# A two-layer model kernel on one core: its routed last pass on paired tiles with five groups added by rows, and its state-space stage written out

## The chip, the cores and the metric

One Trainium2 chip, one of its cores. The metric is the device time of one execution in microseconds (us). TensorE is PE in the profile, VectorE is DVE, ScalarE is ACT, GpSimd is POOL and SyncE is SP. SP and ACT also issue plain DMAs; POOL issues the indirect ones.

## The reference, cut to what matters

The input is x, f32 of shape (2, 4096, 512): 8192 tokens. Four blocks follow each other: a state-space block (projection, causal convolution, selective scan with 16 states per channel, gate, output projection, residual), a sum of eight orthogonal factors with a residual, a decayed linear attention with 16 heads, and a routed spline block. The change rewrites the end of the last one; of the state-space block it changes only how the code is written out:

```python
tile_idx = jnp.argmax(jnp.where(in_cluster, tile_scores, -jnp.inf), axis=-1)   # one of 64 tiles per token
tok_dims = DIMS[tile_idx]                                                      # the 8 features of that tile
x_slice = jnp.take_along_axis(xf, tok_dims, axis=1)
...
mn = tile_min[tile_idx][:, None]; mx = tile_max[tile_idx][:, None]             # over all tokens of the tile
u = jnp.clip((x_slice - mn) / (mx - mn + 1e-08), 0.0, 1.0 - 1e-06)
gi = jnp.clip((u * GRID).astype(jnp.int32), 0, GRID - 1)
b = spline_bases[tile_idx[:, None], j, gi]; s = spline_slopes[tile_idx[:, None], j, gi]
delta = (b + s * (u - gi / GRID) * GRID) * output_scale[tile_idx][:, None]
out = jnp.zeros_like(xf).at[jnp.arange(N)[:, None], tok_dims].set(delta)
return x + out.reshape(B, S, D)
```

The extremes of a tile need every token, so this end can only start when all tokens have been routed.

## The kernel before, in words

The program has three stages, one after the other, each in a block of its own with a barrier of all engines at its end. In all of them every engine's instructions are written out by hand in program order; engines meet by semaphores.

**State-space stage** (`mamba_block`). The sequence is cut in 16 chunks of 512 tokens (8 positions times batch 2). A chunk has 32 steps k; in each, PE builds the input term with `b_product` (L738: 16 matmuls of 32 x 128 weights, four row groups of the array at `tile_position=(32*i, 0)`), ACT the decays (L502), DVE four scans (L652), POOL the product with C (L336), and PE sums over states (L755). Projections, convolution and output projection of the neighbouring chunks lie between the steps by tables of step numbers. `y_out` (L601) of the last pair stands at step 1 of the following chunk. `periods` writes chunks 0, 1, 14 and 15 out and runs chunks 2 to 13 as a hardware loop of six turns with two chunks each, in which every semaphore wait compares with a value computed in registers:

```python
for b in range(BATCH):
    body(0, b, b, b == 0, False)
with eng.Fori(1, NI - 1) as i:
    for b in range(BATCH):
        body(i, b, i * BATCH + b, False, False)
```

**Second stage** (`blocks_after`): 64 tiles of 128 tokens in a software pipeline over the other blocks up to the routing. ACT issues the loads of the constants (18 DMAs, L1141 to L1145), DVE waits for all of them (L1234) and then sums and splits the weights, whose loads SP issues as buffers come free (L1059). It leaves in SBUF the one-hot of each token's tile (`oh_all`, bf16), the 8 picked features (`xs_all`) and the running extremes (`acc`), and stores `out` without the spline's delta (`r_t`, L1080).

**Last pass** (`finish`), L1663 and after, in 16 groups of four tiles:
- PE turns each tile's one-hot (L1803, 64 x 128 out of the 64-column weights), ACT evicts four at a time to `ohT` (L1693, 16 copies), in two alternating banks.
- DVE finds each token's tile number by multiplying the one-hot with 0..63 and reducing (L1701, L1708), so `rows` is known (L1712).
- PE looks up the two extremes of each token's tile (L1815, one matmul with 64-row weights per tile, two columns); DVE turns them into u, the cell and the remainder (L1725 to L1739).
- Per group: PE looks up 128 bases and 128 slopes per token (L1822, 8 matmuls), DVE marks the cells (`mark`, L1750), multiplies with the looked-up rows (`weigh`, L1760), reduces (`pick`, L1767), and forms delta (`slope` L1771, `offset` L1776).
- POOL issues one indirect DMA per tile (L1683), 64 in all, which adds 8 values per token into `out`; each group's four wait for that group's delta.

## Time and profile before

| | us |
|---|---|
| median of 3 executions | 5462.37 (5462.31 to 5465.17) |
| the profiled execution | 5468.6 |
| its span, first to last instruction | 5466.8 |
| state-space stage (0 to the barrier) | 3833 |
| second stage | 3833 to 5288 |
| last pass | 5288 to 5466.8 |

The busy shares over the span are PE 91%, DVE 82%, POOL 58%, ACT 48%. They are averages over three stages that differ, so each part is read in its own stretch. The granted TensorE clock is 1.0 (2.4 GHz) nearly everywhere in the first two stages and 0.5 (1.2 GHz) in the whole last pass. A matmul on f32 has two records in the trace.

### The profile page before, as it was taken

Reading aid. Unit: us, or ns where it says so; the run is one execution under the profiler, and the core shown is the slowest. Engines: PE = TensorE matmul, PEld = TensorE weight load, DVE = VectorE, ACT = ScalarE, POOL = GpSimd, SP = SyncE. Lnnn points to the kernel's source line nnn. Section 1 sums busy time; section 2 is a strip of 40 time slices with the busy share of each in tenths; the row PEclk is TensorE's granted clock in tenths of the full one; section 3 lists DMA queues with packets and bytes.
Section 4 is the critical chain, followed back from the end, with each engine's and each line's share of the span. In section 5 each row is a group of like instructions: output and inputs, shape, how many; then the busy total and the mean of one; then the engine's idle time right before and its main releaser. Section 6 shows DMA issues by size and latency. Waiting matters only on the chain. (4 is left out here: it accounts for less than half of the span.)

```text
span 5466.8 us, 107541 instructions
## 1 busy us (share of the span) xinstructions
PE 4975.0 (91%) x41287; PEld 2967.0 (54%) x41287; DVE 4462.5 (82%) x7277; ACT 2636.9 (48%) x4245; POOL 3175.6 (58%) x1659
## 2 busy tenths in 40 slices
PE   6899999999999999999999999987499999999983
PEld 3345444444444444444444445443388888888863
DVE  3988889888898888889888898886578888888864
ACT  3555556555565655556555565552133333333320
POOL 1676766767667676666766667675144444444427
PEclk9999999999999999999999999998799999999975
DMA  2222212222122222222222222221300000000001
GB/s 83 82 88 81 102 65 101 92 80 101 71 101 80 91 92 75 99 79 93 99 73 100 80 86 97 74 94 68 127 25 27 27 27 27 27 27 27 27 13 2
DMA packets 114433, 384.29 MB, mean 70 GB/s; under 512 B 29184, under 2 KB 30720, under 8 KB 81024
## 3 DMA queue, kind: packets, MB, share of 16 engines
q1 hardware_dynamic: 101600, 373.47, 19.3%
q0 software_dynamic: 9216, 0.27, 0.5%
q8 instruction: 340, 5.57, 0.4%
q10 hardware_dynamic: 3104, 3.58, 0.2%
q14 instruction: 173, 1.42, 0.1%
HBM read 342.92 MB, written 34.34 MB: 69 GB/s over the span
## 5 line engine op out<-in xcount | busy, mean ns | idle before, releaser
L336 POOL TENSOR_TENSOR s<-s,Cb 128x1024 f32<-128x1024 f32 x1024 | 2394.9, 2361 | 1084.2 <-DVE state L657 1073.8
L652 DVE TENSOR_TENSOR_SCAN s<-s,state,BU 128x512 f32<-128x512 f32 x2048 | 2452.8, 1260 | 426.5 <-PE BU L738 393.4
L502 ACT ACTIVATE s<-dt,ch 128x512 f32<-128x512 f32 x2048 | 1305.5, 712 | 780.4 <-PE Y L755 779.0
L755 PE MATMUL Y<-s,ident 64*64 64x512 f32 x8192 | 1014.9, 611 | 76.2 <-POOL s L336 75.2
L684 PE MATMUL PJ<-xnT,w_in 128*128 128x512 f32 x2048 | 946.1, 606 | 9.3 <-ACT dtuT L368 5.7
L738 PEld LDWEIGHTS BU<-spread,dtuT 32*128 32x128 f32 x16384 | 513.3, 189 | 527.7 <-DVE s L652 399.3
L738 PE MATMUL BU<-spread,dtuT 32*128 32x128 f32 x16384 | 611.9, 286 | 144.0 <-DVE s L652 139.6
L684 PEld LDWEIGHTS PJ<-xnT,w_in 128*128 128x128 f32 x2048 | 369.7, 190 | 478.5 <-issue 423.4
L755 PEld LDWEIGHTS Y<-s,ident 64*64 64x64 f32 x8192 | 279.7, 134 | 573.6 <-issue 535.7
L729 PE MATMUL PJ<-w_out,u 128*128 128x512 f32 x1024 | 472.3, 605 | 8.2 <-ACT xnT L372 6.7
L729 PEld LDWEIGHTS PJ<-w_out,u 128*128 128x128 f32 x1024 | 184.9, 190 | 243.3 <-issue 225.5
L1101 POOL TENSOR_TENSOR x1t<-x1t,bias_b 128x512 f32<-128x512 f32 x64 | 83.0, 1297 | 397.6 <-DVE xa L1285 397.6
L545 DVE SCALAR_TENSOR_TENSOR u<-hid,ch,u 128x512 f32<-128x512 f32 x384 | 287.5, 749 | 19.1
L695 PE MATMUL PJ<-w_xp,u 128*128 128x160 f32 x1024 | 252.9, 404 | 9.6 <-issue 6.5
L1106 POOL TENSOR_TENSOR xf<-xf,gamma_b 128x512 f32<-128x512 f32 x64 | 81.7, 1276 | 305.6 <-DVE xf L1472 305.6
L695 PEld LDWEIGHTS PJ<-w_xp,u 128*128 128x128 f32 x1024 | 243.0, 329 | 27.2 <-issue 20.8
L1481 DVE TENSOR_TENSOR scm<-bank,decay 128x512 f32<-128x512 f32 x256 | 159.0, 683 | 70.1 <-PE bank L1590 70.1
L1114 POOL TENSOR_TENSOR qk_all<-rc,rs 128x512 f32<-128x512 f32 x64 | 82.1, 1283 | 170.8 <-DVE rs L1499 170.8
L368 ACT COPY dtuT<-PJ 128x512 f32<-128x512 f32 x128 | 68.8, 588 | 230.6 <-PE PJ L724 230.6
L1551 PE MATMUL bank<-w_high_o,aTs 128*128 128x512 f32 x512 | 179.9, 412 | 0.0
L1551 PE MATMUL bank<-w_high_f,xaT 128*128 128x512 f32 x512 | 177.0, 407 | 1.6 <-DVE xaT L1290 1.4
L1290 DVE TENSOR_TENSOR xaT<-bank,xaT 128x512 fp32r<-128x512 f32 x64 | 44.3, 691 | 161.3 <-ACT xaT L1157 161.3
(238 smaller groups left out, 7095.1 us busy)
## 6 DMA issues: line engine op xcount, KB each, us to landing
Cb<-bc SPq DMA_DIRECT2D x256, 1024.0 KB, 4.8
res<-in_x SPq DMA_DIRECT2D x64, 256.0 KB, 4.8
x<-res SPq DMA_DIRECT2D x64, 256.0 KB, 4.9
x1t<-x SPq DMA_DIRECT2D x64, 256.0 KB, 2.6
out<-r_t SPq DMA_DIRECT2D x64, 256.0 KB, 2.0
xt<-in_x SPq DMA_DIRECT2D x31, 512.0 KB, 5.7
w_in<-in_in_w SPq DMA_DIRECT2D x8, 512.0 KB, 9.6
x_all<-in_factors SPq DMA_DIRECT2D x4, 1024.0 KB, 5.1
```

The source lines that it names most:

```text
L336: nc.gpsimd.tensor_tensor(pair, pair, Cb[q % 2][:, 2 * part * T:2 * part * T + 2 * T], ALU.mult).then_inc(z_ready, 1)
L502: nc.scalar.activation(s[k % SLOTS][:, n, :], dt[p % 2][:, gi, :], ACT.Exp, scale=ch[:, 2 * p + gi, 7 + 4 * nq + n:8 + 4 * nq + n]).then_i ...
L545: last_ = nc.vector.scalar_tensor_tensor(out, h_[:, tap:tap + T], ch[:, m, tap:tap + 1], out, ALU.mult, ALU.add)
L652: nc.vector.tensor_tensor_scan(s[k % SLOTS][:, n, :], s[k % SLOTS][:, n, :], BU[:, n::4], state[:, b, k, n:n + 1], ALU.mult, ALU.add).then ...
L684: last_ = nc.tensor.matmul(bank[:], w_in[:, kb, lo:lo + P], xnT[:, kb, :], start=(kb == 0), stop=(kb == KB - 1))
L695: last_ = nc.tensor.matmul(bank[:, tb % 2 * SP_:(tb % 2 + 1) * SP_], by_block(u[slot][:, g, :])[:, tb], w_xp[:, g, :], start=(g == 0), sto ...
L729: last_ = nc.tensor.matmul(bank[:], u[slot][:, g, j * P:(j + 1) * P], w_out[:, g, :], start=(g == 0), stop=(g == G - 1))
L738: last_ = nc.tensor.matmul(BU[:, i * T:(i + 1) * T].rearrange("p (t b n) -> p b t n", b=TB, n=4)[:, tb], dtuT[rows, gi, tb, :], spread[row ...
L755: last_ = nc.tensor.matmul(Y[r][y_rows(r, gi), :], ident[rows, rows], s[(k_even + gi) % SLOTS][rows, n, :], start=False, stop=(n == 3 and ...
L1101: nc.gpsimd.tensor_tensor(x1t[s_][:], x1t[s_][:], bias_b[:], ALU.add).then_inc(S["x1b_ready"], 1)
L1481: nc.vector.tensor_tensor(scm[:, r, :, :].rearrange("p k n -> p (k n)"), bank(f"sc{r}")[:], decay[:, r, :, :].rearrange("p k n -> p (k n)" ...
L1551: last_ = nc.tensor.matmul(b_[:], src[part][:, k, :], wt, start=(k == 0 and i == 0), stop=(k == KB - 1 and i == 2))
```

## The change

Three edits.

1. `periods` writes all 16 chunks out; the loop is gone, and with it the register values in the waits.
2. The last pass works on pairs of tiles. One matmul turns the one-hots of two tiles, so a transposed block has 128 partitions, tile 2p in partitions 0 to 63 and tile 2p+1 in 64 to 127. The tables (`tab`, `oscale`, the extremes) stand in both halves, and the look-ups alternate between the two row halves of the array (`tile_position=(64*r, 0)`), each half with its own PSUM bank; bases and slopes come from one matmul of 256 columns. The tile number is a third column of the extremes' look-up, which replaces the multiply-and-reduce on DVE. The load of the tables needs two more DMAs on ACT's queue.
3. Groups 11 to 15 are no longer scattered. SP reads their rows of `out` (10 DMAs of 512 KB) at the start of the pass, DVE spreads delta over the 512 features by the one-hot (`to_rows`) and adds (`add_rows`), and SP stores the rows. POOL issues 44 indirect DMAs.

The buffers of the last pass are allocated anew after the second stage's are released.

```diff
         def periods(eng, body):
 
-            for b in range(BATCH):
-                body(0, b, b, b == 0, False)
-            with eng.Fori(1, NI - 1) as i:
-                for b in range(BATCH):
-                    body(i, b, i * BATCH + b, False, False)
-            for b in range(BATCH):
-                body(NI - 1, b, (NI - 1) * BATCH + b, False, b == BATCH - 1)
+            for c in range(NCH):
+                body(c // BATCH, c % BATCH, c, c == 0, c == NCH - 1)
...
-            act.dma_start(tab[:, 0, :], w["bases"].rearrange("a j g -> a (j g)")).then_inc(S["w_loaded2"], 16)
-            act.dma_start(tab[:, 1, :], w["slopes"].rearrange("a j g -> a (j g)")).then_inc(S["w_loaded2"], 16)
+            for h in range(2):
+                both = slice(NTILE * h, NTILE * h + NTILE)
+                for q, src in enumerate(("bases", "slopes")):
+                    act.dma_start(tab[both, q, :], w[src].rearrange("a j g -> a (j g)")).then_inc(S["w_loaded2"], 16)
...
-            dve.wait_ge(S["w_loaded2"], 16 * 18)
+            dve.wait_ge(S["w_loaded2"], 16 * 20)
...
+    BY_ROWS = 5
+    SCATTERED = GROUPS - BY_ROWS
...
+        @block.sync
+        def _(sp):
+            for i in range(BY_ROWS):
+                for b in range(2):
+                    sp.dma_start(rows_of[i][:, b::2, :],
+                                 out_v[b, of_group(SCATTERED + i)].rearrange("i p d -> p i d")).then_inc(rows_loaded, 16)
+            for i in range(BY_ROWS):
+                sp.wait_ge(rows_added, i + 1)
+                for b in range(2):
+                    sp.dma_start(out_v[b, of_group(SCATTERED + i)].rearrange("i p d -> p i d"),
+                                 rows_of[i][:, b::2, :]).then_inc(rows_stored, 16)
+            sp.wait_ge(rows_stored, 32 * BY_ROWS)
 
         @block.gpsimd
...
-            for t in range(TILES):
+            for t in range(SCATTERED * N):
-            pool.wait_ge(scattered, 16 * TILES)
+            pool.wait_ge(scattered, 16 * SCATTERED * N)
...
-            nc.scalar.copy(ident_b[:], ident[:]).then_inc(ident_ready, 1)
-            for g in range(GROUPS):
-                act.wait_ge(oh_turned, g + 1)
-                nc.scalar.copy(ohT(g * N, N), banks[g % 2][0:NTILE, :]).then_inc(ohT_ready, 1)
+            for h in range(GROUPS // 2):
+                act.wait_ge(oh_turned, h + 1)
+                nc.scalar.copy(ohT(h * N, N), banks[h % 2][:]).then_inc(ohT_ready, 1)
...
+            nc.vector.tensor_copy(ident_b[:], ident[:]).then_inc(ext_column, 1)
+            for q in range(2):
+                nc.vector.tensor_copy(twice[:, q, :].rearrange("p (h i) -> p h i", h=2),
+                                      ident[:, q * NTILE:(q + 1) * NTILE].unsqueeze(1).to_broadcast([P, 2, NTILE])
+                                      ).then_inc(ext_column, 1)
+            nc.vector.tensor_copy(ext[:, 2:3], tile_no[:]).then_inc(ext_column, 1)
...
-            half = TILES // 2
-            for h in range(2):
-                nc.vector.tensor_tensor(
-                    marked[h][:].rearrange("p k (t i) -> p (k t) i", i=NTILE), oh[:, h * half:(h + 1) * half, :],
-                    buf["tile_no"][:].unsqueeze(1).to_broadcast([P, half, NTILE]), ALU.mult).then_inc(marked_ready, 1)
             dve.wait_ge(ext_full, 1)
-            nc.vector.tensor_copy(ext[:], banks[6][0:NTILE, 0:2]).then_inc(ext_ready, 1)
-            for h in range(2):
-                dve.wait_ge(marked_ready, h + 1)
-                nc.vector.tensor_reduce(idx[:, h * half:(h + 1) * half],
-                                        marked[h][:].rearrange("p k (t i) -> p (k t) i", i=NTILE), AX.X, ALU.add
-                                        ).then_inc(idx_step, 1)
-            dve.wait_ge(idx_step, 2)
-            nc.vector.tensor_tensor(rows[:], idx, buf["row_base"][:], ALU.add).then_inc(rows_ready, 1)
+            nc.vector.tensor_copy(ext[:, 0:2], banks[7][:, P:P + 2]).then_inc(ext_ready, 1)
 
             steps = itertools.count(1)
...
+            for r in range(2):
+                nc.vector.tensor_copy(e[:, r, :], banks[6 + r][:, 0:3 * TILES // 2]).then_inc(chain, 1)
+                next(steps)
+            dve.wait_ge(chain, 2)
+            e_q = e[:].rearrange("p r (t q) -> p t r q", q=3)
+            by_pair = rdn[:].rearrange("p (t r) -> p t r", r=2)
+            nc.vector.tensor_tensor(rows[:].rearrange("p (t r) -> p t r", r=2), e_q[:, :, :, 2],
+                                    row_base[:].rearrange("p (t r) -> p t r", r=2), ALU.add).then_inc(rows_ready, 1)
+            then(nc.vector.tensor_tensor(by_pair, e_q[:, :, :, 0], e_q[:, :, :, 1], ALU.add))
+            then(nc.vector.tensor_scalar_add(rdn[:], rdn[:], 1e-8))
+            for r in range(2):
+                def half(ap):
+                    return per_dim(ap).rearrange("p (t r) j -> p t r j", r=2)[:, :, r, :]
+                nc.vector.tensor_tensor(half(v16[:]), xs[:].rearrange("p (t r) j -> p t r j", r=2)[:, :, r, :],
+                                        e_q[:, :, r, 1].unsqueeze(2).to_broadcast([P, TILES // 2, DS]), ALU.add)
+            then(nc.vector.reciprocal(rdn[:], rdn[:]))
+            then(nc.vector.tensor_tensor(per_dim(v16[:]), per_dim(v16[:]), spread(rdn[:]), ALU.mult))
...
-            def weigh(g, q):
-                if q == 0:
+            def weigh(g, r):
+                if r == 0:
                     dve.wait_ge(eq_ready, g + 1)
...
-                nc.vector.tensor_tensor(prod[q][:], eq[g % 2][:], banks[2 * (g % 2) + 2 + q][:], ALU.mult
-                                        ).then_inc(prod_ready, 1)
-
-            def pick(g, q):
-                dve.wait_ge(prod_ready, 2 * g + 1 + q)
+                    dve.wait_ge(picked, 2 * (g - 1) + 1 + r)
+                marks = eq[g % 2][:].rearrange("p (t r c) -> p t r c", r=2, c=P)[:, :, r, :]
+                nc.vector.tensor_tensor(prod[r][:].rearrange("p (t q c) -> p t q c", q=2, c=P),
+                                        marks.unsqueeze(2).to_broadcast([P, 2, 2, P]),
+                                        banks[2 * (g % 2) + 2 + r][:].rearrange("p (t q c) -> p t q c", q=2, c=P),
+                                        ALU.mult).then_inc(prod_ready, 1)
...
+            def to_rows(g):
+                i = g - SCATTERED
+                if i >= 2:
+                    dve.wait_ge(rows_added, i - 1)
+                dve.wait_ge(delta_ready, g + 1)
+                nc.vector.tensor_tensor(od[i % 2][:].rearrange("p t (i j) -> p t i j", j=DS),
+                                        oh[:, g * N:(g + 1) * N, :].unsqueeze(3).to_broadcast([P, N, NTILE, DS]),
+                                        per_dim(of(delta, g)).unsqueeze(2).to_broadcast([P, N, NTILE, DS]), ALU.mult
+                                        ).then_inc(od_ready, 1)
+
+            def add_rows(g):
+                i = g - SCATTERED
+                dve.wait_ge(rows_loaded, 32 * BY_ROWS)
+                dve.wait_ge(od_ready, i + 1)
+                nc.vector.tensor_tensor(rows_of[i][:], rows_of[i][:], od[i % 2][:], ALU.add).then_inc(rows_added, 1)
...
                     offset(g - 1)
                 pick(g, 1)
+                if g > SCATTERED:
+                    to_rows(g - 1)
+                if g > SCATTERED + 1:
+                    add_rows(g - 2)
             slope(GROUPS - 1)
+            add_rows(GROUPS - 2)
             offset(GROUPS - 1)
+            to_rows(GROUPS - 1)
+            add_rows(GROUPS - 1)
 
...
-            for g in range(GROUPS):
-                if g >= 2:
-                    pe.wait_ge(ohT_ready, g - 1)
-                for t in range(g * N, (g + 1) * N):
-                    last_ = nc.tensor.matmul(banks[g % 2][0:NTILE, t % N * P:(t % N + 1) * P], oh[:, t, :], ident_b[:],
+            pe.wait_ge(ext_column, 1)
+            for h in range(GROUPS // 2):
+                if h >= 2:
+                    pe.wait_ge(ohT_ready, h - 1)
+                for n in range(N):
+                    pair = h * N + n
+                    last_ = nc.tensor.matmul(banks[h % 2][:, n * P:(n + 1) * P],
+                                             oh[:, 2 * pair:2 * pair + 2, :].rearrange("p t i -> p (t i)"), ident_b[:],
                                              start=True, stop=True)
                 last_.then_inc(oh_turned, 1)
-                if g == 1:
-                    pe.wait_ge(ext_column, 1)
+                if h == 1:
+                    pe.wait_ge(ext_column, 5)
                     for q in range(2):
-                        last_ = nc.tensor.matmul(banks[6][0:NTILE, q:q + 1], ident[:, q * NTILE:(q + 1) * NTILE],
-                                                 ext_T[:], start=True, stop=True)
+                        last_ = nc.tensor.matmul(banks[7][:, P + q:P + q + 1], twice[:, q, :], ext_T[:],
+                                                 start=True, stop=True)
                     last_.then_inc(ext_full, 1)
             pe.wait_ge(ext_ready, 1)
-            pe.wait_ge(ohT_ready, GROUPS)
-            for t in range(TILES):
-                last_ = nc.tensor.matmul(banks[6][:, 2 * t:2 * t + 2], ohT(t), ext[:], start=True, stop=True)
+            pe.wait_ge(ohT_ready, GROUPS // 2)
+            pe.sem_inc(pe_steps3, 1)
+            for pair in range(TILES // 2):
+                for r in range(2):
+                    half = slice(NTILE * r, NTILE * r + NTILE)
+                    last_ = nc.tensor.matmul(banks[6 + r][:, 3 * pair:3 * pair + 3], ohT(pair)[half, :], ext[half, :],
+                                             start=True, stop=True, tile_position=(NTILE * r, 0))
             last_.then_inc(e_full, 1)
             for g in range(GROUPS):
                 if g >= 2:
                     pe.wait_ge(prod_ready, 2 * (g - 2) + 2)
-                for q in range(2):
-                    for t in range(N):
-                        last_ = nc.tensor.matmul(banks[2 * (g % 2) + 2 + q][:, t * P:(t + 1) * P], ohT(g * N + t),
-                                                 tab[:, q, :], start=True, stop=True)
+                    pe.sem_inc(pe_steps3, 1)
+                for n in range(2):
+                    for r in range(2):
+                        half = slice(NTILE * r, NTILE * r + NTILE)
+                        last_ = nc.tensor.matmul(banks[2 * (g % 2) + 2 + r][:, 2 * n * P:2 * n * P + 2 * P],
+                                                 ohT(2 * g + n)[half, :], tab[half].rearrange("a q c -> a (q c)"),
+                                                 start=True, stop=True, tile_position=(NTILE * r, 0))
                 last_.then_inc(looked_up, 1)
```

On PE, the last pass from the transpose of the extremes on; before:

```order
L1796 MATMUL bank<-ident,acc 128x128
L1803 MATMUL bank<-x1t,oh_all 64x128 x8
L1809 MATMUL bank<-x1t,ident 64x1 x2
L1803 MATMUL bank<-x1t,oh_all 64x128 x56
L1815 MATMUL bank<-x1t,x_all 128x2 x16
L1815 MATMUL bank<-x1t,qk_all 128x2 x16
L1815 MATMUL bank<-x1t,scm 128x2 x16
L1815 MATMUL bank<-x1t,decay 128x2 x16
L1822 MATMUL bank<-tab,x_all 128x128 x32
L1822 MATMUL bank<-tab,qk_all 128x128 x32
L1822 MATMUL bank<-tab,scm 128x128 x32
L1822 MATMUL bank<-tab,decay 128x128 x32
```

and now:

```order
L1854 MATMUL bank<-ident,acc 128x128
L1862 MATMUL bank<-ident_b,oh_all 128x128 x8
L1869 MATMUL bank<-ext_T,twice 128x1 x2
L1862 MATMUL bank<-ident_b,oh_all 128x128 x24
L1878 MATMUL bank<-ext,ohT 128x3 x64
L1888 MATMUL bank<-tab,ohT 128x256 x64
```

The 64 transposes are 32, the extremes' look-ups keep their number and read three columns, and the 128 look-ups of the tables are 64 of twice the columns.

On DVE, the end of the last pass, from the second `weigh` and the last reductions on; before:

```order
L1767 TENSOR_REDUCE kTs<-xb 128x32
L1760 TENSOR_TENSOR xb<-xa,bank 128x512
L1771 TENSOR_TENSOR kTs<-kTs,x_0 128x32
L1760 TENSOR_TENSOR xb<-xa,bank 128x512
L1767 TENSOR_REDUCE kTs<-xb 128x32
L1776 TENSOR_TENSOR rc<-kTs 128x32
L1767 TENSOR_REDUCE kTs<-xb 128x32
L1771 TENSOR_TENSOR kTs<-kTs,x_0 128x32
L1776 TENSOR_TENSOR rc<-kTs 128x32
```

and now (`od` is delta spread to rows, `rows_of` the rows of `out`):

```order
L1805 TENSOR_TENSOR sel<-sel,v 128x4x8
L1790 TENSOR_TENSOR prod<-eq,bank 128x512
L1799 TENSOR_REDUCE sel<-prod 128x32
L1810 TENSOR_TENSOR delta<-sel 128x2x2x8
L1799 TENSOR_REDUCE sel<-prod 128x32
L1819 TENSOR_TENSOR od<-oh_all,delta 128x2048
L1828 TENSOR_TENSOR rows_of<-rows_of,od 128x2048
L1805 TENSOR_TENSOR sel<-sel,v 128x4x8
L1828 TENSOR_TENSOR rows_of<-rows_of,od 128x2048
L1810 TENSOR_TENSOR delta<-sel 128x2x2x8
L1819 TENSOR_TENSOR od<-oh_all,delta 128x2048
L1828 TENSOR_TENSOR rows_of<-rows_of,od 128x2048
```

Behind the group's own instructions stand products and sums of 2048 elements a partition, five of each in all; they are behind `pick` of groups 12 to 15 and at the end.

## Rows read from the trace of the kernel before

**Rows 1.** the page, its first line

```profile
span 5466.8 us, 107541 instructions
```

**Rows 2.** busy time by window: chunks 2 to 13, second stage, last pass

```profile
core 0: us, PE busy (x) PEld busy (x) DVE busy (x) ACT busy (x) POOL busy (x), PEclk, DMA share, GB/s
581.00:3349.00 2768.00, 2625.57 (x22753) 1301.29 (x22752) 2417.15 (x2941) 1632.46 (x2388) 1887.64 (x853) 1.00 0.25 88
3833.00:5288.00 1455.00, 1342.31 (x10498) 1121.82 (x10498) 1169.10 (x3225) 446.60 (x1027) 558.26 (x452) 0.96 0.11 36
5288.00:5467.00 179.00, 92.12 (x453) 89.05 (x453) 67.84 (x132) 8.79 (x17) 100.30 (x64) 0.50 0.15 2
```

**Rows 3.** timeline, DVE: gate multiply of chunks 1, 2, 3, 14, 15

```profile
362.07 1.26 DVE L601 TENSOR_TENSOR u<-Y,gate 128x512 f32<-128x512 f32 x2
591.48 1.26 DVE L601 TENSOR_TENSOR u<-Y,gate 128x512 f32<-128x512 f32 x2
821.67 1.26 DVE L601 TENSOR_TENSOR u<-Y,gate 128x512 f32<-128x512 f32 x2
...
3359.56 1.26 DVE L601 TENSOR_TENSOR u<-Y,gate 128x512 f32<-128x512 f32 x2
3588.68 1.26 DVE L601 TENSOR_TENSOR u<-Y,gate 128x512 f32<-128x512 f32 x2
```

**Rows 4.** the page: a queue that fetches instructions (packets, MB, share)

```profile
q8 instruction: 340, 5.57, 0.4%
```

**Rows 5.** timeline, ACT in the last pass: first and last evictions of one-hots

```profile
5289.28 1.06 ACT L1693 COPY x_all<-bank 64x512 f32<-64x512 f32 x2 [0.78 <-PE bank L1803]
...
5298.40 1.06 ACT L1693 COPY decay<-bank 64x512 f32<-64x512 f32 x2 [0.24 <-PE bank L1803]
```

**Rows 6.** groups by form: a quarter of the look-ups of the extremes

```profile
L1815 PE MATMUL bank<-x1t,scm 64*128 64x2 f32 x32 | 7.0, 349 | 0.0
```

**Rows 7.** timeline, PE: one 32-row tiled product of 16 matmuls at half clock

```profile
133.57 2.09 PE L738 MATMUL BU<-spread,dtuT 32*128 32x128 f32 x32 [4.99 <-DVE s L652]
```

**Rows 8.** timeline, DVE: range extremes arriving, last step before marking, group pace

```profile
5327.07 0.29 DVE L1725 COPY kTs<-bank 128x128 f32<-128x128 f32 x1 [28.96 <-PE bank L1815]
5333.82 1.29 DVE L1750 TENSOR_TENSOR xa<-x,grid 128x512 f32<-128x512 f32 x2
5340.61 0.68 DVE L1750 TENSOR_TENSOR xa<-x,grid 128x512 f32<-128x512 f32 x1
5343.79 0.68 DVE L1750 TENSOR_TENSOR xa<-x,grid 128x512 f32<-128x512 f32 x1
```

**Rows 9.** timeline, scatters: first two, a slow one, its mark, the last

```profile
5341.04 1.85 POOL L1683 DMA_INDIRECT out<-rc,x1t  x1 [59.63 <-DVE rc L1776]
5343.19 1.55 POOL L1683 DMA_INDIRECT out<-rc,x1t  x1 [0.30 <-issue]
...
5359.90 0.68 DVE L1750 TENSOR_TENSOR xa<-x,grid 128x512 f32<-128x512 f32 x1
5359.98 2.02 POOL L1683 DMA_INDIRECT out<-rc,x1t  x1 [0.30 <-issue]
...
5455.10 1.56 POOL L1683 DMA_INDIRECT out<-rc,x1t  x1 [2.00 <-issue]
5460.68 1.55 POOL L1683 DMA_INDIRECT out<-rc,x1t  x1 [0.30 <-issue]
```

**Rows 10.** groups of instructions by line, DVE, weight set-up (busy us, mean ns)

```profile
L1258 DVE TENSOR_TENSOR qk_all<-qk_all,scm 128x2048 f32<-128x2048 f32 x4 | 9.2, 2292 | 2.9 <-DMA scm<-in_factors 2.8
```

**Rows 11.** timeline, second stage: last constant load, and DVE's wait for it

```profile
3843.72 0.61 ACTq L1145 DMA_DIRECT2D tab<-in_slopes  x1
3850.10 0.28 DVE L1235 TENSOR_REDUCE smean<-tab 64x8 f32<-64x128 f32 x1 [19.55 <-DMA tab<-in_slopes]
```

**Rows 12.** DMA issues by line (KB each, median us to landing)

```profile
out<-r_t SPq DMA_DIRECT2D x64, 256.0 KB, 2.0
x_all<-in_factors SPq DMA_DIRECT2D x4, 1024.0 KB, 5.1
```

More of the change, by code:

```diff
@@ L898, in blocks_after, with keep @@
     ctx = ExitStack()
+    stage = ExitStack()
     with ctx:
         def sb(name, shape, dt=F32):
+            return stage.enter_context(nc.sbuf_tensor(name, shape, dt))
+        def keep(name, shape, dt=F32):
             return ctx.enter_context(nc.sbuf_tensor(name, shape, dt))
@@ L1644, in finish @@
[L1644 removed]
+        stage.close()
+        finish(nc, out, out_v, banks, dict(ident=ident, tab=tab, grid16=grid16, acc=acc, oh=oh_all, xs=xs_all,
+                                           row_base=row_base, tile_no=tile_no), NTILE, DS, GRID, TILES)
+def finish(nc, out, out_v, banks, kept, NTILE, DS, GRID, TILES):
     N = 4
     GROUPS = TILES // N
[L1648 to L1651 removed]
+    BY_ROWS = 5
+    SCATTERED = GROUPS - BY_ROWS
+    ident, tab, grid16, acc, oh, xs, row_base, tile_no = (
+        kept[n] for n in ("ident", "tab", "grid16", "acc", "oh", "xs", "row_base", "tile_no"))
@@ L1664, in sem @@
         def sem(name):
             return ctx.enter_context(nc.semaphore(name))
[L1667 to L1671 removed]
+        CELLS = TILES * DS
@@ new lines, in finish @@
+        ohT_all = [sb(f"ohT{i}", [P, TILES // 4 * P]) for i in range(2)]
+        rows_of = [sb(f"rows_of{i}", [P, N, NTILE * DS]) for i in range(BY_ROWS)]
+        od = [sb(f"od{i}", [P, N, NTILE * DS]) for i in range(2)]
+        eq, prod = ([sb(f"{n}{i}", [P, N * P]) for i in range(2)] for n in ("eq", "prod"))
+        v16, gf, gt, delta = (sb(n, [P, CELLS]) for n in ("v16", "gf", "gt", "delta"))
+        gi, rows = sb("gi", [P, CELLS], I32), sb("rows", [P, TILES], I32)
+        ident_b = sb("ident_b", [P, P], BF16)
```

89 lines of the change are left out of this document (39 added, 50 removed).

## The prediction

> **What bounds the kernel now.** I read the page's first line, then busy time by window, then the timeline of each stretch that the change touches. The span is 5466.8 us [rows 1]. Three stages follow each other behind barriers [rows 2], so what is saved in one is saved at the end.
>
> *State-space stage.* In chunks 2 to 13 PE is busy 2625.6 of 2768 us and DVE 2417 [rows 2]. The engines take turns in each step, so I don't look for one bound but for a yardstick: the gate multiply in step 1 of each chunk, one period apart. Chunks 1 and 14 are written out already, chunks 2 to 13 run in the loop. From chunk 1's row to chunk 2's is 229.41 us, from 14's to 15's 229.12; in the loop the first period is 230.19, and the twelve take 3359.56 - 591.48 = 2768.08 us, 230.67 each [rows 3].
>
> *Last pass.* PE and DVE have done most of it by 5387 us; from the first scatter at 5341.04 to the last one's end (5460.68 + 1.55 = 5462.23) POOL issues its 64 indirect DMAs, 1.55 us each with 0.30 between them [rows 9]. So the pass is a prologue of 53 us up to the first delta (barrier at 5288), then POOL's queue for 121.2 us, then 4.6 us of landing and ending. TensorE has 1.2 GHz throughout it [rows 2].
>
> **The change, part by part.**
>
> *Loop written out.* Nothing is computed differently; register arithmetic before the waits and the branch go. The price is read off the same code without a loop: the mean of the two written-out periods is 229.27, the loop's 230.67, so 12 x 1.40 = **-17 us** (by chunk 1 alone -15, by chunk 14 alone -19).
>
> *Two more loads in the second stage.* DVE waits for the last constant, 19.55 us of idle time ended by that load, which ACT issued at 3843.72 after one every half microsecond [rows 11]. Two more issues of about 0.6 come ahead of it, and the weights' setup hangs on that wait: **+1.2 us** (0 if another load would be last).
>
> *Transposes of one-hots.* 16 evictions take 5289.28 to 5298.40 + 1.06 = 5299.46 [rows 5], 0.64 each; PE and ACT alternate on two banks. Now there are 8; 128 columns of weights instead of 64 hide beside the 128 columns that pass, and an eviction of 128 partitions costs what one of 64 does. 5.1 us, and 0.3 for the longer product of the extremes that stands between: **-4.8**. The multiply and reduction of tile numbers lay beside this; with them gone nothing is won.
>
> *Look-ups of the extremes.* A quarter, 16 matmuls in 32 records, takes 7.0 us [rows 6], all 64 take 27.4; nothing else runs on the path. There are still 64, now alternating between row halves. How two halves overlap no row of this shape shows. Bounds: no overlap, 0 gained, and full overlap, 13.7. The nearest row: 16 matmuls of 32-row weights in four row groups take 2.09 us at the same clock [rows 7], 0.13 each against 0.44, 3.3 times as fast with four groups, loading of weights included. I take the full factor two for two groups: **-13.6**.
>
> *DVE up to the first delta.* From the extremes' arrival (5327.07) to the first mark (5333.82) it is a chain of short dependent operations [rows 8]. One copy becomes two, an addition for the row numbers and a second half-sized addition come in: **+0.5**. First mark and first delta follow as before. The first scatter is thus due at 5341.04 - 4.8 - 13.6 + 0.5 = 5323.1 (in the old time scale).
>
> *POOL.* 44 scatters at 1.85 us are 81.4, less the last gap 81.1. To this comes what DVE costs POOL. Of the 24 scatters issued while DVE works, most take 1.55 us, but one that starts 0.08 after a mark began takes 2.02 [rows 9]: it ends late by about what the mark had left. A mark has both inputs in SBUF; multiplies that read PSUM and reductions delay nothing. The new `to_rows` and `add_rows` have both inputs in SBUF, and 2048 elements of f32 take 2.29 us [rows 10], longer than POOL's 1.85 rhythm, so no scatter can slip between. They come mostly in pairs: a scatter that starts inside the first waits about 1.1 on average, the next falls into the second one's end and waits about 0.4. Five pairs, 7.5 us, and 1.5 for the marks. 81.1 + 9 = 90.1 against 121.2: **-31.1**. The 2.00 us pause before the 61st scatter [rows 9] is in the 121.2 and is assumed not to come with 44.
>
> The Trainium skill (SBUF — State Buffer, Who interferes with whom) says that a DVE instruction with two SBUF inputs contends with a GpSimd instruction that reads SBUF, and that the second to issue fully blocks; by that rule the trace agrees (2.02 against 1.55). The same page's warning on software-generated DMAs names only the two-port copies of DVE; by that alone `to_rows` and `add_rows` would cost POOL nothing, and the sum would be 7.5 us lower.
>
> *DVE's own end.* A group costs it 3.18 us (5340.61 to 5343.79) [rows 8]. First mark at 5333.82 - 17.9 = 5315.9, 16 groups 50.9, ten long operations at 2.21 net 22.1: 5389. PE's look-ups, 4 matmuls of 256 columns a group, take 3.4 us if the halves don't overlap and 1.7 if they do, so they hold DVE up little or not at all. The store of the last group, two DMAs of 512 KB, lands within 5.1 us (1 MB took that) [rows 12]: 5395. The last scatter ends at 5323.1 + 90.1 = 5413.2. POOL stays the bound, with 18 us of slack for DVE and SP. The 5 MB of rows read at the start take 5 x 5.1 = 26 us [rows 12], done by 5315 and first wanted after 5360. If scatters were free of DVE, the slack would still be 9 us.
>
> *Sum.* -17 + 1.2 - 4.8 - 13.6 + 0.5 - 31.1 = -64.8 us. The profiled execution took 5468.6 us, 1.8 over its span and 6.2 above the median of 5462.4; it becomes 5403.8, the median **5398 us**.
>
> **The rivals.**
>
> A. *Row halves do not overlap.* For: each f32 matmul passes twice (two records) through its own half before the next half's is issued, and no row has two row groups of 128 columns. Against: the four-group product. +13.6 on the path: 5411.
>
> B. *The long DVE operations don't hold POOL.* For: the evidence is a few scatters on one kind of instruction. Against: the delay follows the mark's remaining time. -7.5: 5390.
>
> C. *POOL is shut out over a whole pair*, since DVE's next operation is queued when the first ends. Marks were followed by PSUM readers, so the trace can't say. Another 2.2 us per pair less what the second wait already costs, five times, about +9: 5407.
>
> D. *Chunks 2 to 13 are slow for another reason than the loop.* For: chunks 1 and 14 lie at the ends. Against: the same instructions with registers in every wait. +17: 5415.
>
> E. *Slower than before: written-out code starves for instructions.* The larger fetch queue moved 5.57 MB in 340 packets [rows 4]; written out, the stage brings the code of ten more chunks that no turn repeats. If fetches were exposed, each of the 12 chunks would lose time; the kernel becomes slower by over 0.2% once a chunk loses (64.8 + 11) / 12 = 6.3 us against the loop-free 229.3. With 8 us each it would be 5494. Against: chunks 1 and 14 are fetched fresh, with no such loss, and the whole second stage is written out.
>
> **How the numbers follow.** What I forecast has 0.56, A 0.10, B 0.12, C 0.12, D 0.05, E 0.03; 0.02 is left for something that undoes the pass's gain altogether. The predicted time is the likeliest case's, 5398. Its own uncertainties are 2 us on the loop, 3 on how the scatters fall against DVE's operations, 2 on the pause: about 6. The range takes in B below and A and C above: 5385 to 5412. A difference under 0.2%, 11 us, is about what a measurement of this kernel cannot tell from none. All cases but E, and part of the last, are faster by more: faster 0.96, same 0.01, slower 0.03.
>
> **What the profile of the changed kernel would show.** Gate multiplies 229.1 to 229.4 us apart in all chunks; if 230.7, the loop was not the cause. The second stage about 1 us longer. Eight evictions in some 5.5 us; 64 look-ups of three columns in 13.8 us (A: 27.4). First scatter some 35 us after the barrier, not 53. Scatters of 1.55 us, and in the last third of DVE's work five or more of 2 to 3.5 us that start inside `to_rows` or `add_rows` (B: none; C: up to 5). DVE done about 24 us ahead of the last scatter. If the last store lands after the last scatter, or POOL waits for a delta, my reading of the bound is wrong.

## The result and the profile after

The changed kernel takes 5411.12 us (median of 4 runs, 5409.99 to 5414.31), the kernel before, run beside it, 5463.69 (4 runs, 5462.31 to 5465.17). The ratio is 0.9901, 95% interval 0.9888 to 0.9913: 52.6 us are gained. The prediction was 5398 with a range of 5385 to 5412, a gain of 64.4. The profiled execution took 5414.31 us.

First the page of the changed kernel, its span and its instruction queue (packets, MB, share), to be held against [rows 1, 4]:

```profile
span 5412.4 us, 102320 instructions
...
q8 instruction: 328, 5.37, 0.4%
```

Busy time by window, the three stretches that answer to [rows 2], moved to where the stages now lie:

```profile
core 0: us, PE busy (x) PEld busy (x) DVE busy (x) ACT busy (x) POOL busy (x), PEclk, DMA share, GB/s
581.00:3349.00 2768.00, 2640.32 (x22924) 1309.88 (x22923) 2436.72 (x2963) 1643.85 (x2404) 1901.05 (x860) 1.00 0.25 89
3813.00:5275.00 1462.00, 1348.96 (x10498) 1121.98 (x10499) 1171.32 (x3225) 446.58 (x1027) 557.32 (x452) 0.96 0.11 36
5275.00:5413.00 138.00, 51.67 (x293) 38.16 (x293) 80.95 (x144) 4.29 (x8) 84.21 (x44) 0.51 0.34 78
```

The second window spoils the forecast. The same number of matmuls (10498) and of DVE instructions (3225) fills 1462 us, where it filled 1455. Beyond the two loads, priced at 1.2 us, nothing that the diff above shows explains it.

*State-space stage.* The timeline of DVE, gate multiplies of chunks 1, 2, 3, 14 and 15, against [rows 3]:

```profile
362.48 1.26 DVE L596 TENSOR_TENSOR u<-Y,gate 128x512 f32<-128x512 f32 x2
591.65 1.26 DVE L596 TENSOR_TENSOR u<-Y,gate 128x512 f32<-128x512 f32 x2
821.05 1.27 DVE L596 TENSOR_TENSOR u<-Y,gate 128x512 f32<-128x512 f32 x2
...
3339.87 1.26 DVE L596 TENSOR_TENSOR u<-Y,gate 128x512 f32<-128x512 f32 x2
3568.72 1.27 DVE L596 TENSOR_TENSOR u<-Y,gate 128x512 f32<-128x512 f32 x2
```

The twelve chunks that the loop ran take 3339.87 - 591.65 = 2748.22 us, 229.02 each, against 2768.08 and 230.67. Code loading did not grow: 5.37 MB in 328 packets over the whole execution, against 5.57 MB in 340.

*Last pass up to the first scatter.* ACT's evictions (timeline), the look-ups of the extremes (groups by form, from 5275 to 5303), and DVE's first copy and first mark (timeline), against [rows 5, 6, 8]:

```profile
5275.95 1.07 ACT L1720 COPY ohT<-bank 128x512 f32<-128x512 f32 x2 [7.09 <-PE bank L1862]
...
5280.15 1.07 ACT L1720 COPY ohT<-bank 128x512 f32<-128x512 f32 x2 [0.21 <-PE bank L1862]
```

```profile
L1878 PE MATMUL bank<-ext,ohT 64*128 64x3 f32 x128 | 13.8, 350 | 0.7 <-issue 0.7
```

```profile
5295.18 0.42 DVE L1747 COPY e<-bank 128x96 f32<-128x96 f32 x2 [17.89 <-PE bank L1878]
...
5302.32 1.29 DVE L1778 TENSOR_TENSOR eq<-gf,grid 128x512 f32<-128x512 f32 x2
```

Eight evictions end at 5281.2 and 64 look-ups take 13.8 us instead of 27.4, a full factor of two. The look-ups alternate between two row halves and, with them, between two PSUM banks, where all wrote one bank before; no run separates the two.

*Last pass, scatters.* The timeline of POOL, first two scatters and last, against [rows 9]:

```profile
5309.52 1.86 POOL L1711 DMA_INDIRECT out<-delta,rows  x1 [41.32 <-DVE delta L1810]
5311.69 1.54 POOL L1711 DMA_INDIRECT out<-delta,rows  x1 [0.30 <-issue]
...
5405.29 1.54 POOL L1711 DMA_INDIRECT out<-delta,rows  x1 [0.30 <-issue]
```

From the first to the end of the last it is 97.3 us; 44 scatters without any wait would be 81.1. The 16.2 us that are missing come from places such as this one, in the timeline around one group by rows:

```profile
5348.77 1.54 POOL L1711 DMA_INDIRECT out<-delta,rows  x1 [0.30 <-issue]
...
5349.53 2.30 DVE L1819 TENSOR_TENSOR od<-oh_all,delta 128x2048 f32<-128x2048 bf16 x1
5350.62 5.44 POOL L1711 DMA_INDIRECT out<-delta,rows  x1 [0.30 <-issue]
5351.73 2.31 DVE L1828 TENSOR_TENSOR rows_of<-rows_of,od 128x2048 f32<-128x2048 f32 x1
5353.93 0.71 DVE L1778 TENSOR_TENSOR eq<-gf,grid 128x512 f32<-128x512 f32 x1
...
5354.53 0.70 DVE L1790 TENSOR_TENSOR prod<-eq,bank 128x512 f32<-128x512 f32 x1
...
5356.36 1.54 POOL L1711 DMA_INDIRECT out<-delta,rows  x1 [0.30 <-issue]
```

One scatter takes 5.44 us. It starts within `to_rows`, sits through `add_rows` and the mark behind it, and ends 1.42 us after the mark has ended (5354.64, against 5356.06): nearly a whole scatter's time after the end of the run (a row of operations with both inputs in SBUF, each of which starts some 0.1 us before the one ahead has ended). The next operation, which reads PSUM, doesn't disturb it.

Where the span went, before to after:

| stretch | before | after | change | predicted |
|---|---|---|---|---|
| end of the last scan | 3791.3 | 3771.3 | -20.0 | -17 |
| from there to the last pass's first transpose | 1496.9 | 1503.7 | +6.8 | +1.2 |
| to the first scatter | 52.8 | 34.5 | -18.3 | -17.9 |
| first scatter to the last one's end | 121.2 | 97.3 | -23.9 | -31.1 |
| to the end | 4.6 | 5.6 | +1.0 | 0 |
| span | 5466.8 | 5412.4 | -54.4 | -64.8 |

### The profile page after: what moved, and what is told of

It reads as the page before. It is cut to its first block and busy times, and to the rows that moved or that the text cites. A ratio compares the mean times of both kernels' runs of the same rounds, so it can differ in the third digit from the quotient of the medians.

```text
span 5412.4 us, 102320 instructions
## 1 busy us (share of the span) xinstructions
PE 4936.5 (91%) x41127; PEld 2916.7 (54%) x41127; DVE 4479.3 (83%) x7289; ACT 2633.0 (49%) x4236; POOL 3157.2 (58%) x1639
## 3 DMA queue, kind: packets, MB, share of 16 engines
q8 instruction: 328, 5.37, 0.4%
```

## Finding the second stage's 6 us

The second stage ran as a pipeline over 64 tiles. The timeline of DVE gives a mark once a tile, the statistics of a new tile. Tiles 8 and 56 in the kernel before:

```profile
4033.52 0.68 DVE L1273 BATCH_NORM_STATS2 st_a<-x1t 128x6 f32<-128x512 f32 x1
...
5043.89 0.68 DVE L1273 BATCH_NORM_STATS2 st_a<-x1t 128x6 f32<-128x512 f32 x1
```

and in the changed kernel:

```profile
4014.22 0.68 DVE L1274 BATCH_NORM_STATS2 st_a<-x1t 128x6 f32<-128x512 f32 x1
...
5029.59 0.68 DVE L1274 BATCH_NORM_STATS2 st_a<-x1t 128x6 f32<-128x512 f32 x1
```

That is (5043.89 - 4033.52) / 48 = 21.05 us a tile before and 21.15 after, evenly in all tiles. The granted clock is the same (0.96 in the windows). The tenth of a microsecond is found on PE, whose queue is full here (busy for 1003 of the 1015 us between these two tiles). In the kernel before, the 12 matmuls of the product for k start at even steps (timeline of PE):

```profile
4521.64 0.39 PE L1551 MATMUL bank<-w_high_k,xbT 128*128 128x512 f32 x1
4521.86 0.39 PE L1551 MATMUL bank<-w_low_k,xbT 128*128 128x512 f32 x1
...
4524.35 0.39 PE L1551 MATMUL bank<-w_high_v,xbT 128*128 128x512 f32 x1
```

and in the changed kernel the same 12 take 2.75 us, not 2.71:

```profile
4504.78 0.39 PE L1552 MATMUL bank<-w_high_k,xbT 128*128 128x512 f32 x1
4505.01 0.39 PE L1552 MATMUL bank<-w_low_k,xbT 128*128 128x512 f32 x1
...
4507.53 0.39 PE L1552 MATMUL bank<-w_high_v,xbT 128*128 128x512 f32 x1
```

Averaged over 43 tiles, the steps of the q product were 226.7, 226.6 and 226.6 ns (high to low, low to high, high to high) and are 225.8, 229.2 and 231.7: 6.8 ns for each three matmuls, some 0.08 us over the 36 of q, k and v in a tile. The instructions are the same. What the change did touch, in lines that the diff above leaves out, is where the tensors lie: the eight that outlive the stage are now allocated ahead of the weights, which moves the weights up by 12640 bytes, but `ones` and what follows it, the transposed blocks among them, by less, since ident, tab and grid16 no longer lie between. The blocks moved by 11040. Four of the experiments below are on this.

## The experiments

All are timed in five rounds beside the kernel before, whose median was 5464.9 us beside `pad_new`, `pad_old`, `unroll_only` and `no_rows`, 5465.9 beside `addr_old`, `dist_new`, `spread_rows` and `psum_od`, and 5466.7 beside `pieces` and the last two. Since the first stage alone ends up to 5 us apart from run to run of the same code, I read each cause from its own stretch of the trace and use the whole time only as a second witness.

**pad_new: everything 32 bytes higher.** Before the change the weights began at a multiple of 64 bytes, after it 32 bytes beside one.

```diff
         tile_no = keep("tile_no", [P, 1])
+        keep("pad", [P, 8])
```

> The changed kernel with 32 unused bytes allocated behind tile_no, so that every tensor of the second stage starts 32 bytes higher, at a multiple of 64 bytes as before the change (w_high_f at 29184 instead of 29152). Alignment theory: the q, k and v products start every 226.6 ns again instead of 225.8, 229.2 and 231.7 ns, each of the 64 pipeline tiles takes 21.05 us instead of 21.15, and the program gets 6 to 6.5 us faster, 5405 us. Rival, the cost lies in which tensors lie beside each other or in the instructions' own order: the tiles keep 21.15 us and the time stays at 5411.

5411.09 us, ratio 0.9899 (0.9884 to 0.9915): nothing gained. A tile takes 21.17 us, as long as in the changed kernel. The three steps of the q product became 231.5, 225.9 and 229.2 ns: the same three values with their places exchanged, the same sum. Addresses do something here, but alignment to 64 bytes is not it.

**pad_old: the kernel before, 32 bytes higher.**

```diff
+        sb("pad", [P, 8])
         w_high, w_low = ({n: sb(f"w_{part}_{n}", [P, KB, HID], F32R) ...
```

> The kernel before with 32 unused bytes allocated ahead of w_high_f, everything else as it was. Alignment theory: each of the 64 tiles takes 21.15 us instead of 21.05 and the program is 6 to 6.5 us slower, 5470 us. Rival as for the other padding: nothing changes, 5463.7 us.

5466.08 us, ratio 1.0002 (0.9993 to 1.0011), 21.05 us a tile, 226.7 ns a step. The theory of alignment fell in this direction too.

**unroll_only: the kernel before with `periods` written out.**

```diff
-            for b in range(BATCH):
-                body(0, b, b, b == 0, False)
-            with eng.Fori(1, NI - 1) as i:
...
+            for c in range(NCH):
+                body(c // BATCH, c % BATCH, c, c == 0, c == NCH - 1)
```

> The kernel before with only the state-space stage unrolled. Theory: the last scan ends 20 us earlier, as in the changed kernel, the second stage keeps its 21.05 us a tile and the last pass its length, so the program is 20 us faster, 5443.5 us. Rival, the unrolled instructions cost the second stage its 6 us (instruction supply): the gain is 14 us, 5450 us.

5444.96 us, ratio 0.9962 (0.9949 to 0.9976), 19.9 us less than before. The twelve chunks take 2747.4 us (2748.2 in the changed kernel), and the second stage keeps 21.05 us a tile and its steps of 226.6 ns. So neither a longer code nor where PE's instructions lie costs the 6 us.

**addr_old: the kernel before with the second stage's tensors where the changed kernel has them,** all up to the late ones behind `ts`. Instructions change in nothing but their addresses.

```diff
+        ident = sb("ident2", [P, P])
+        tab = sb("tab", [NTILE, 2, DS * GRID])
+        grid16 = sb("grid16", [P, GRID])
...
+        row_base = sb("row_base", [P, TILES])
+        sb("pad", [P, 1])
         w_high, w_low = ({n: sb(f"w_{part}_{n}", [P, KB, HID], F32R) ...
...
```

> The kernel before with its tensors allocated in the changed kernel's order, so that w_high_f starts at 29152, xbT0 at 158368 and all others of the second stage up to ts where they do in the changed kernel; no instruction changes but its addresses. Placement theory (which survives the failed padding: it is the distance between tensors that counts, not a multiple of 64 bytes): the tiles take 21.15 us instead of 21.05, 5471 us. Rival, the cost lies in the instruction streams of the changed kernel's second stage: the tiles keep 21.05 us, 5464.5 us.

5472.15 us, 6.3 more than before, ratio 1.0011 (1.0002 to 1.0020). The timeline of DVE, tiles 8 and 56:

```profile
4030.16 0.68 DVE L1274 BATCH_NORM_STATS2 st_a<-x1t 128x6 f32<-128x512 f32 x1
...
5045.52 0.68 DVE L1274 BATCH_NORM_STATS2 st_a<-x1t 128x6 f32<-128x512 f32 x1
```

21.15 us a tile, and steps of 226.0, 229.1 and 231.6 ns: the changed kernel's rate without any other part of the change. From the first tile's statistics to the last one's the profiled execution took 4.4 us more than the kernel before, the changed kernel 6.1; stretches of the same placement differ by up to 2 us from run to run, and the steady rate between tiles 8 and 56 is the firmer witness.

**dist_new: the changed kernel with the old distance from the weights to the transposed blocks.** Everything from rms_w on moves 1600 bytes up, away from the weights.

```diff
+        pr = sb("pr", [P, HID], BF16)
+        cs = sb("cs", [P, 8])
+        cm = sb("cm", [P, 8])
+        cand = sb("cand", [P, 2, NTILE])
         rms_w = sb("rms_w", [P, KB])
...
```

> The changed kernel with 1600 bytes of tensors that were allocated late (pr, cs, cm, cand) allocated between w_low_o and rms_w, so that the distance from each weight to x1t, xaT, xbT, aTs and everything between them is what it was before the change, all of them 12640 bytes higher. If the distance from the weights to the transposed blocks decides: 21.05 us a tile, 5405 us. If the addresses themselves decide, or the order of instructions: 21.15 us, 5411 us.

5404.53 us, 61.4 below the kernel before, ratio 0.9889 (0.9874 to 0.9905). Tiles 8 and 56:

```profile
4010.46 0.68 DVE L1274 BATCH_NORM_STATS2 st_a<-x1t 128x6 f32<-128x512 f32 x1
...
5021.37 0.68 DVE L1274 BATCH_NORM_STATS2 st_a<-x1t 128x6 f32<-128x512 f32 x1
```

21.06 us a tile, all steps 226.7 ns. So it is the placement, shown in both directions, and it goes with the distance between the weights and the rest. Which pair of tensors, and which distances are bad, was not tried; that the blocks' own address matters, beyond 32 bytes, is not excluded.

**no_rows: no group by rows,** that is 64 scatters and none of the rows' loads, operations and stores.

```diff
-    BY_ROWS = 5
+    BY_ROWS = 0
...
```

> The changed kernel with no group by rows: 64 scatters, no loads, additions and stores of rows. If the port waits come from the row operations: 64 scatters at 1.85 us are 118.4 us, the waits at the marks 9 us as before the change and one pause of 2 us, 129 us from first to last against 97.3, so the last pass and the program are 32 us longer, 5443 us. If the waits have another cause (they come with GpSimd's own queue) there are as many per scatter as now, 16 us for 44 or 23 us for 64, and the program takes 5457 us.

5433.16 us, ratio 0.9942 (0.9928 to 0.9956). Neither number of mine is met, as I had counted the port waits of the kernel before at 9 us. They are small: the 64 scatters take 121.1 us from the first to the end of the last, 3.0 more than 64 without a wait, and half of that is one pause (timeline of POOL):

```profile
5302.33 1.86 POOL L1713 DMA_INDIRECT out<-delta,rows  x1 [41.33 <-DVE delta L1812]
...
5412.89 1.55 POOL L1713 DMA_INDIRECT out<-delta,rows  x1 [0.30 <-issue]
5416.27 1.56 POOL L1713 DMA_INDIRECT out<-delta,rows  x1 [1.83 <-issue]
...
5421.85 1.55 POOL L1713 DMA_INDIRECT out<-delta,rows  x1 [0.30 <-issue]
```

So the five groups by rows are worth 121.1 - 97.3 = 23.8 us: 20 scatters less, 37.0 us, and 13.2 us more of waiting. The waits come with the row operations. The stretch behind the last scatter is 4.7 us long here, against 5.6 in the changed kernel.

**spread_rows: the row operations kept apart.**

```diff
                 weigh(g, 1)
-                pick(g, 0)
                 if g > 0:
                     offset(g - 1)
-                pick(g, 1)
                 if g > SCATTERED:
                     to_rows(g - 1)
+                pick(g, 0)
                 if g > SCATTERED + 1:
                     add_rows(g - 2)
+                pick(g, 1)
```

> The changed kernel with the last pass's row operations kept apart on VectorE: to_rows before pick of the first half, add_rows between the two picks, instead of both behind the second pick and in front of the next mark. Theory (GpSimd is kept out for a whole run of adjacent operations with two SBUF inputs): the waits of single scatters of 3.3 to 5.7 us go, none is above 2.3 us, their sum falls from 16.2 us to about 9, the last scatter is issued 6 to 7 us earlier, 5405 us. Rival (each of the ten row operations costs its own time, wherever it stands): the sum stays at 14 to 16 us and the time at 5410.

5406.47 us, ratio 0.9891 (0.9875 to 0.9906). The longest scatter is now 3.42 us, not 7.24, but ten of them take more than 2 us, not six, and the waits sum up to 12.0 us, between the two theories. The timeline of POOL and DVE shows why it is no less:

```profile
5348.72 2.28 DVE L1828 TENSOR_TENSOR rows_of<-rows_of,od 128x2048 f32<-128x2048 f32 x1
5349.93 2.49 POOL L1711 DMA_INDIRECT out<-delta,rows  x1 [0.30 <-issue]
```

The addition ends at 5351.00, the scatter at 5352.42: again 1.42 us later. A single operation makes a scatter that starts within it pay all that is left of the operation. Adjacency is only the worse case of it.

**psum_od: the products in PSUM.**

```diff
+            od_banks = [banks[n] for n in (0, 1, 6, 7)]
...
+                for n in range(N):
+                    last_ = nc.vector.tensor_tensor(rows_of[i][:, n, :], rows_of[i][:, n, :], od_banks[n][:], ALU.add)
...
```

> The changed kernel with the products of to_rows kept in PSUM (banks 0, 1, 6 and 7, four operations of 512 columns each), so that add_rows reads one input from SBUF and one from PSUM, as weigh does. Theory: the additions no longer keep GpSimd out, half of the row operations' waits go, 16.2 to about 8 us, 5403 us. Rival (a long operation on VectorE keeps it out whatever it reads): 16 us stay, and the shorter pieces cost VectorE a little, 5411 us.

The edit also turns the order round, `add_rows` of the group before now stands ahead of `to_rows`, and `to_rows` waits for the additions before it.

5396.69 us, ratio 0.9875 (0.9860 to 0.9890). The last scatter ends 84.3 us after the first began, 3.2 of it waits. More than the additions' half is gone. Its timeline of POOL and DVE:

```profile
5346.01 1.54 POOL L1710 DMA_INDIRECT out<-delta,rows  x1 [0.30 <-issue]
5347.44 2.51 DVE L1821 TENSOR_TENSOR bank<-oh_all,delta 128x512 f32<-128x512 bf16 x4
5347.86 1.69 POOL L1710 DMA_INDIRECT out<-delta,rows  x1 [0.30 <-issue]
...
5353.09 2.46 DVE L1832 TENSOR_TENSOR rows_of<-rows_of,bank 128x512 f32<-128x512 f32 x4
5353.55 1.54 POOL L1710 DMA_INDIRECT out<-delta,rows  x1 [0.30 <-issue]
```

A scatter within the additions takes its 1.54 us, and so do all 21 that start within additions in this run and the last two below. But the products, which still read two SBUF tensors and now write PSUM in four pieces, hold this one up by only 0.15.

**pieces: four short operations, products still in SBUF.** The PSUM version had changed length, place and order at once; this one has the length alone.

```diff
...
+                for n in range(N):
+                    last_ = nc.vector.tensor_tensor(rows_of[i][:, n, :], rows_of[i][:, n, :], od[i % 2][:, n, :], ALU.add)
...
```

> The changed kernel with to_rows and add_rows cut into four operations of 512 columns each, their products still in SBUF. It separates the two things that the PSUM version changed at once. If the length of one operation decides (GpSimd slips in between short ones): the waits fall to about 3 us in all as with PSUM, the last scatter is issued 13 us earlier than in the changed kernel, 5397 us. If it is the number of inputs from SBUF in a run of adjacent operations, whatever their length: the eight short operations of a group still keep GpSimd out for 4.6 us and more, the waits stay at 15 to 18 us, 5411 us.

5410.81 us, ratio 0.9899 (0.9884 to 0.9914), as the changed kernel. The waits are 17.1 us; the worst, in the timeline:

```profile
5359.49 2.52 DVE L1820 TENSOR_TENSOR od<-oh_all,delta 128x512 f32<-128x512 bf16 x4
5360.60 7.86 POOL L1711 DMA_INDIRECT out<-delta,rows  x1 [0.30 <-issue]
5361.90 2.53 DVE L1831 TENSOR_TENSOR rows_of<-rows_of,od 128x512 f32<-128x512 f32 x4
```

So it is not length: chains of 0.7 us operations with both inputs in SBUF keep GpSimd out as the long ones did; these too start some 0.1 us before the one ahead has ended. What frees GpSimd during the additions is that they read one input from PSUM. That doesn't hold of the products, whose inputs are the same in both versions.

**rows6_psum and rows7_psum: products in PSUM, the old distances, and six or seven groups by rows.**

```diff
...
-    BY_ROWS = 5
+    BY_ROWS = 6
...
```

> The changed kernel with products in PSUM, the distances between tensors of the kernel before, and six of 16 groups by rows. GpSimd: 40 scatters, 7.4 us less than 44, so its last one is issued 7 us earlier; VectorE: one group's row operations more, 5 us, ends about 5378 less the 9 us of placement and of the earlier start. Sum against the changed kernel: 14.4 (PSUM) + 6.6 (placement) + 6 to 7, 5384 us. Rival, VectorE and the last store set the end already: 5387 us.

5384.31 us, ratio 0.9849 (0.9835 to 0.9862), as expected, though VectorE ended at 5375.7 and not near 5369. One scatter took 3.44 us. It starts 0.49 us after a product that writes PSUM began and ends 1.42 us after the mark behind the products (timeline of DVE and POOL):

```profile
5334.42 3.44 POOL L1710 DMA_INDIRECT out<-delta,rows  x1 [0.30 <-issue]
5335.73 0.71 DVE L1777 TENSOR_TENSOR eq<-gf,grid 128x512 f32<-128x512 f32 x1
```

The seven:

> The same with seven groups by rows. GpSimd has 36 scatters and would end another 7.4 us earlier, but VectorE ends 5 us later than with six and its last store lands some 4 us after it: both ends lie within 2 us, and the time is that of six groups within 3 us, 5382 to 5387 us. If VectorE is the later one by more than that, it is slower than with six.

5382.73 us, ratio 0.9848 (0.9835 to 0.9862). With six the last scatter still ends last (5379.5, VectorE 5375.7); with seven it ends at 5370.0 and VectorE is the later one (timeline of DVE, last additions):

```profile
5375.83 2.48 DVE L1832 TENSOR_TENSOR rows_of<-rows_of,bank 128x512 f32<-128x512 f32 x4
```

The spans, 5384.7 and 5382.9 us, are within 2 us of each other, and the times of the two versions overlap (5382.64 to 5386.57 and 5382.08 to 5386.32). Seven has the lowest median tried: 83.9 us less than the kernel before, 31 more than the change gains by itself.

## Why the prediction came out as it did

*The loop, -17 predicted, -20.0 found.* The mechanism was right and shown alone by `unroll_only`. The size came from the two written-out chunks before, 229.27 us on average; written out, the twelve take 229.02, and the chunk after them 228.85 instead of 229.12, which the prediction left as it was. Rivals D (another cause) and E (starving for instructions) are refuted: no chunk is slower and the queue fetched less.

*Second stage, +1.2 predicted, +6.8 found.* The step that failed is "Two more loads in the second stage" as the only term for it. The loads cost even less: DVE's wait on the last constant went from 19.55 to 19.73 us, and the first tile starts 0.3 us later, counted from the last scan. From the first tile to the last it is 6.1 us more, and behind the last 0.4. The 6.1 us are the placement of tensors (the allocations moved to `keep`), which I priced at nothing without saying so. Here the kernel's queue on PE is full, so 2 to 5 ns on a matmul reach the end of the stage.

*Up to the first scatter, -17.9 predicted, -18.3 found.* Transposes, look-ups at full overlap and DVE's chain came out as forecast, first scatter 34.5 us after the barrier. Rival A (no overlap) is refuted by 13.8 us for 64 look-ups. The nearest row, four row groups in one product [rows 7], was a good guide.

*POOL, -31.1 predicted, -23.9 found.* Here "the next falls into the second one's end and waits about 0.4" failed. In the changed kernel no scatter is let in at the seam of two operations that overlap by 0.1 us: rival C, with its place and nearly its price (+9 given, 16.2 - 9 = 7.2 found), except that the run can be longer than a pair and single scatters then take up to 7.24 us, not 5. The measure for a single operation held. [rows 9] was read as "it ends late by about what the mark had left": the mark ends at 5360.58 and the scatter at 5362.00, 1.42 us later, the same 1.42 as after the runs in the changed kernel, and a scatter that has 0.60 us of a mark ahead of it is thus late by 0.48. What failed is to what the measure was applied: to each operation, where it belongs to the whole run. A run of 2.3 + 2.3 + 0.7 us costs a scatter that starts early in it up to 5 us. Rival B is refuted.

On the Trainium skill (SBUF — State Buffer, Who interferes with whom): its rule that a DVE instruction with two SBUF inputs contends with a GpSimd instruction that reads SBUF, and that the other then fully blocks, is borne out here for scatters, 5.44 us against 1.54. The same page's warning for software-generated DMAs names only two-port copies, and the section infers that a `tensor_tensor` leaves the writing of descriptors alone; `to_rows`, `add_rows` and the marks are such operations, and the measured 5.44 us decides against that. By its rule the products of `psum_od` should hold GpSimd as those of `pieces` do, wherever they write. Of the five scatters that met them one took 2.93 us (a mark stood behind them), the others 1.65 to 1.94: they were let in when the product in which they had started ended, and ended 1.41 us after it. With six groups one took 3.44 us and with seven one 4.27; these end, like the 2.93, 1.42 us after the mark behind the products, so the products can hold a scatter as those in SBUF do. The moment seems to decide, not the place of the output. All 13 scatters that start 0.41 to 0.46 us after a product began were let in at its end, one of them in `pieces`, where the products lie in SBUF. The four at 0.49 to 0.51 us were held to the end of the run, three in `pieces` and one with six groups. But two at 0.17 and 0.21 us were let in as well, and three at 0.26, 0.37 and 0.40 were held. That was not tried by itself and stays open. How much of the 13 us is owed to PSUM can be estimated from the three long waits of `pieces`: had only the products held them, they would have ended 1.42 us after 5346.61, 5354.62 and 5362.02, 10.4 us earlier in all. The rest would be the moment.

*The two ends.* DVE's end was forecast at 5389 in the old time scale; less the 13.2 us by which the pass began earlier that is 5375.8, and there it ended. DVE was done 31 us ahead of the last scatter, not 24, since the scatters waited longer. The last store was no bound, as foreseen. The 1.0 us more after the last scatter goes with the row groups (4.7 us in `no_rows`, 4.6 before the change); why is not shown.

The sum of the errors is -3.0 + 5.6 - 0.4 + 7.2 + 1.0 = 10.4 us, the difference between -64.8 and -54.4. Between the medians the gain fell short by 11.8 us, 52.6 against 64.4. The result lies 0.9 us inside the upper edge of the range, and that it does is partly luck. The edge of 5412 stood there for rival A at 5411, which is refuted, more than for rival C at 5407, which came true; the second stage's 5.6 us had no place in it, and only the loop's 3 us made up for a part.

## What to carry to other kernels

Price an added VectorE operation by what it does to GpSimd's queue too: where both its inputs were in SBUF, a scatter mostly waited for the end of the whole run of such operations and then still needed 1.42 of its 1.54 us. Put one input in PSUM; cutting the operations up didn't help here (17.1 us of waits against 16.2), and spreading them out helped a little (12.0). A diff that moves allocations moves addresses in stages that it doesn't otherwise touch; in a stage with a full PE queue compare the steps between matmuls before and after. And when two queues share one job, move the split until both end together: after each repair it was worth moving again.

## What was not expected of the hardware

Equal matmuls of 128x128 by 128x512 f32 follow each other at 226.6 ns or at 225.8, 229.2 and 231.7 ns depending on nothing but where the stage's tensors lie in SBUF: 6.1 us over 64 tiles. A shift of all by 32 bytes exchanges the three values and keeps their sum. After a run of DVE operations with two SBUF inputs a waiting scatter ends 1.42 us later (those of 5.44, 4.83 and 7.24 us all do), of the 1.54 that it takes undisturbed. A tenth of a microsecond between two long operations let it in, and then the next one didn't stop it: near the end of the pass one ends while `add_rows` runs (timeline of DVE and POOL, changed kernel).

```profile
5371.13 2.29 DVE L1819 TENSOR_TENSOR od<-oh_all,delta 128x2048 f32<-128x2048 bf16 x1
5372.75 2.09 POOL L1711 DMA_INDIRECT out<-delta,rows  x1 [0.30 <-issue]
5373.52 2.29 DVE L1828 TENSOR_TENSOR rows_of<-rows_of,od 128x2048 f32<-128x2048 f32 x1
```

The products end at 5373.42, the additions begin at 5373.52, and the scatter ends at 5374.84. With the state-space stage written out, the execution fetched slightly less code on this queue (5.39 MB in `unroll_only`) than with its loop (5.57 MB).
